# Loading the query and key stacks three groups ahead instead of two in a transformer kernel

## What is computed

```
x = x + cross_attention0(norm(x), ctx, mask)          # 16 heads of 16 features
x = x + block0(norm(x))     # self-attention (16 heads), then 8 experts of 1024 hidden units
x = x + cross_attention1(norm(x), ctx)                # no mask
x = x + experts1(norm(x))   # gate over 256 columns, 8 experts of 256 x 256
```

## Time and profile before

| | us |
|---|---|
| median of 3 runs (lowest, highest) | 1280.65 (1279.75, 1281.99) |
| the profiled execution's own time | 1274.43 |
| its span, first to last instruction | 1272.7 |
| TensorE busy | 1131.4 (89%) |
| VectorE busy | 838.6 (66%) |
| ScalarE busy | 660.4 (52%) |
| GpSimd busy | 210.9 (17%) |
| mean granted TensorE clock | 0.949 of full |

### The profile page before, as it was taken

One profiled execution on the slowest core, in us unless ns is written; L12 is line 12 of the kernel. 1 busy time (PEld: TensorE's weight loads), 2 busy tenths in 40 slices (PEclk: granted clock), 3 DMA queues, 4 the chain that ended last, 5 costly groups with the idle time before them and its releaser, 6 DMA issues. The chain is left out here.

```text
span 1272.7 us, 17810 instructions
## 1 busy us (share of the span) xinstructions
PE 1131.4 (89%) x5693; PEld 544.0 (43%) x5722; DVE 838.6 (66%) x2112; ACT 660.4 (52%) x1341; POOL 210.9 (17%) x272
## 2 busy tenths in 40 slices
PE   7889999999997999999967999996989999998390
PEld 4423343434453223343364666664523333335370
DVE  5878777777478888888762222223888888876722
ACT  3346666666533677677722333332537767674250
POOL 4310000000143000000202222211520010102154
PEclk9989999999999899999967999998989999999795
DMA  8953321221048433543291140103873323211064
GB/s 265 309 169 93 79 57 28 81 52 26 2 154 291 103 91 90 132 97 93 72 375 33 31 161 28 27 13 102 263 241 91 90 59 89 60 37 57 25 171 144
DMA packets 100706, 139.40 MB, mean 110 GB/s; under 512 B 8452, under 2 KB 82632, under 8 KB 99208
## 3 DMA queue, kind: packets, MB, share of 16 engines
q1 hardware_dynamic: 96536, 128.03, 33.6%
q0 software_dynamic: 4080, 10.23, 2.9%
HBM read 86.30 MB, written 52.17 MB: 109 GB/s over the span
## 5 line engine op out<-in xcount | busy, mean ns | idle before, releaser
L885 ACT ACTIVATE r<-ps 128x512 f32<-128x512 f32 x768 | 427.4, 600 | 211.9 <-PE ps L971 122.1
L377 DVE TENSOR_REDUCE m<-ps 128x1 f32<-128x512 f32 x512 | 320.9, 682 | 45.2 <-PE ps L958 44.9
L971 PE MATMUL ps<-r 99*128 99x512 bf16 x768 | 294.3, 388 | 5.6 <-ACT r L885 5.6
L958 PE MATMUL ps<-r 96*128 96x512 bf16 x720 | 280.9, 393 | 20.5 <-DVE m L377 7.0
L373 DVE CUSTOM_DVE_ANT_0 r<-ps,r 128x512 bf16<-128x512 f32 x256 | 170.2, 690 | 60.2 <-PE ps L958 59.6
L985 PE MATMUL ps<-r 128*32 128x512 f32 x1536 | 204.9, 605 | 4.9 <-ACT r L885 3.3
L971 PEld LDWEIGHTS ps<-r 99*128 99x128 bf16 x768 | 74.4, 98 | 211.7 <-ACT r L885 157.3
L958 PEld LDWEIGHTS ps<-r 96*128 96x128 bf16 x720 | 71.3, 99 | 105.9 <-DVE m L377 24.3
L861 POOL COPY r<-r 128x256 f32<-128x256 f32 x48 | 19.0, 399 | 542.1 <-PE ps L985 542.1
L1660 DVE COPY r<-ps 128x512 f32<-128x512 f32 x46 | 31.8, 691 | 91.9 <-PE ps L1707 91.9
L1707 PE MATMUL ps<-r 128*128 x184 | 87.8, 621 | 2.7 <-issue 0.4
(11 more groups left out here) (151 smaller groups left out, 1220.5 us busy)
## 6 DMA issues: line engine op xcount, KB each, us to landing
r<-q_parts SPq DMA_DIRECT2D x48, 384.0 KB, 5.2
r<-k_parts SPq DMA_DIRECT2D x48, 384.0 KB, 6.0
k_parts<-r SPq DMA_DIRECT2D x24, 384.0 KB, 3.3
q_parts<-r SPq DMA_DIRECT2D x24, 384.0 KB, 3.1
r<-in_w SPq DMA_DIRECT2D x16, 512.0 KB, 4.9
r<-in_w SPq DMA_DIRECT2D x8, 1024.0 KB, 14.4
k_parts<-r SPq DMA_DIRECT2D x24, 256.0 KB, 3.3
q_parts<-r SPq DMA_DIRECT2D x24, 256.0 KB, 3.1
```

Source lines behind the costliest of these rows:

```text
L377: ins = dve.tensor_reduce(out, mem.ps[:, bank, :], AX.X, ALU.max)
L885: act.activation(mem.probs[:, u // HG, u % HG, :], ps[:, ST + (UNITS * g + u) % DEEP, :], ACT.Exp, scale=SCALE).then_inc(a.p_exp.sem, 1)
L958: pe.matmul(ps[:, led_bank(n), :], mem.qst[g][0:ROWS, h, t * P:(t + 1) * P], mem.kst[g][0:ROWS, h, :], start=True, stop=True).then_inc(a.s ...
L971: ins = pe.matmul(out, mem.kst[g][0:KROWS, h, kt * P:(kt + 1) * P], mem.qst[g][0:KROWS, h, :], start=True, stop=not a.masked)
```

## The change

The stacks are loaded three groups ahead. In the projection phase a third group's stacks are loaded beside the first two. In the attention phase step 1 of group G loads the stacks of group G + 3; its wait is for the transposed scores of group G - 1, whose buffers these are, and for G = 0 there is no wait. So that step now comes when group G - 1 has ended, and the shift of group G + 1 is issued behind it. The wait for the last stores of the projection moves with it to g = 1 of the first batch. No load is added or left out over a stage.

```diff
         for n in range(QK):
             sp.wait_ge(a.stored[n].sem, a.stored[n].at(1))
-        load_stacks(sp, a, 0, 0)
-        load_stacks(sp, a, 0, 1)
+        for g in range(AHEAD):
+            load_stacks(sp, a, 0, g)
         body(B - 2, None)
         body(B - 1, None)
...
+AHEAD = 3
...
         for g in range(NG):
             G = NG * b + g
-            ahead = (b, g + 2) if g < 2 else (b + 1, g - 2)
-            if not (last and g >= 2):
-                if first and g == 2:
+            ahead = (b, g + AHEAD) if g + AHEAD < NG else (b + 1, g + AHEAD - NG)
+            if not (last and g + AHEAD >= NG):
+                if first and g + AHEAD == NG:
                     for n in range(QK):
                         sp.wait_ge(a.stored[n].sem, a.stored[n].at(B))
-                if not (first and g < 2):
-                    sp.wait_ge(a.st_ps.sem, a.st_ps.at(G - 1))
+                if G + AHEAD >= NG:
+                    sp.wait_ge(a.st_ps.sem, a.st_ps.at(G + AHEAD - NG + 1))
                 load_stacks(sp, a, *ahead)
```

## The result

| | before | changed |
|---|---|---|
| median, us (lowest to highest) | 1279.75 (1276.92 to 1281.99), 7 runs | 1284.56 (1283.51 to 1286.37), 7 runs |
| ratio, 95% interval | | 1.0040 (1.0026 to 1.0054) |
| span of the profiled execution, us | 1272.7 | 1282.2 |
| mean granted TensorE clock there | 0.949 | 0.945 |

The change costs 4.8 us in the medians. The two profiled executions lie 9.5 us apart, since that of before is one of its quicker ones; so the places are read from the profiles and the size from the medians. The page's engine row, which answers to the earlier trace rows: the same work. The 7 us more of busy TensorE are in part a gap in the record: the profile of before lacks 29 matmuls of its line 975 (x5693 against x5722), and two profiles of experiments 1 and 7, which have all 5722, show 1134.7 and 1135.3.

What follows compares the result with a forecast made beforehand. PE was taken to bound the attention phases and DVE the end of each projection phase. A gain of 5.2 us and a cost of 6.5 made +1.3, 1281.9 us from a median of 1280.65; whole range 1276.0 to 1286.5.

Steps and rivals of the forecast that it cites:

- all twelve waits go: Attention phases: loads issued 8 units sooner end all twelve waits of plain scores for the stack loads of line 334.
- the wait put into SP's queue: Attention phase, SP's queue: the new wait for the end of group G - 1 was put at nothing.
- the gain of 5.2 us: Attention phases: worth of the twelve removed waits, measured between matmul starts less cadence; bounds 3.4 and 7.6 us.
- Rival C: Attention phases: removed waits come back as waits for ACT or DVE; gain 2 us or less, time 1285, chance 0.15.
- the third pair's bytes hold up batch 2's stores: Projection phases: 768 KB ahead of the stores delay them 3.1 us a stage; 6.5 us together on the path.
- Rival A: Projection phases: the last batch's first-piece stores are not late, gain without cost; time 1275.4, chance 0.20.
- 11 us to land: Projection phases, a sign: stores behind the loads take about 11 us to land, 8.5 in the second stage.
- SP's longer issuing: Projection phases: two more DMAs, about 1.0 us to issue, costed at nothing; at most 1.0 a stage if engines run dry.
- rival B: Last projection batch: PE's clock falls in the pause, 5 to 7.5 us a stage; 1287 if in one stage; chance 0.13.
- the likeliest case: Whole kernel: the forecast itself, -5.2 + 6.5 = +1.3 us, 1281.9, own range 1277.5 to 1284.5, chance 0.52.
- "The same": Whole kernel: measured time within 0.2%, 2.6 us, of the kernel before; chance 0.42.
- "slower": Whole kernel: slower than the kernel before by over 0.2%, 2.6 us; chance 0.32.

Runs made afterwards that it cites:

- experiment 1: Changed kernel with the third pair of stacks loaded at the start of the attention phase, behind the first shift; 1275.29 us, ratio 0.9978 to the kernel before.
- experiment 7: Changed kernel with only the first pair of stacks ahead of batch 2's stores, second and third behind them; 1274.40 us, ratio 0.9973 to the kernel before.
- experiment 5: Against experiment 1's kernel: two loads of 24 KB each in the projection phase, in the early third pair's place; 1275.09 us, ratio 0.9977 to the kernel before.
- experiment 6: Changed kernel with the fourth group's stacks also loaded in the projection phase, no load at group 0; 1294.56 us, ratio 1.0132 to the kernel before.
- experiment 3: Changed kernel with TensorE doing the last batch's second key projection twice, to fill the pause; 1279.41 us, ratio 1.0009 to the kernel before.
- experiment 8: Experiment 7's kernel with the third plain score ahead of each attention phase issued 13 times; 1275.22 us, ratio 0.9977 to the kernel before.

## Why the prediction was right in part and wrong in part

- **Right: all twelve waits go.** Line 334 has no plain score waiting, and the wait put into SP's queue costs nothing (experiment 1).
- **Mis-sized: the gain of 5.2 us.** It measured 3.84 from group 1 on in the profiles and 2.8 in the medians of experiment 1. I had written that the start of the matmuls "say when the work behind can go". They do not: each wait removed uncovers about 0.2 us of waiting for DVE's bank. Rival C, that the waits come back, is true for a quarter of the gain in the profiles and for nearly half of it by the medians.
- **Right: the third pair's bytes hold up batch 2's stores, and ACT, then DVE, wait for them in all three stages.** The awaited store landed 2.9 and 3.1 us later in stages 1 and 3, against the 3.1 of a pair. Rival A, that the stores are not late, falls. Experiments 5 and 6 bear out size and dose. For the wait alone 2.45, 1.4 and 2.7 were expected, 6.5 together; the changed kernel shows 2.01, 1.66 and 2.98, 6.65. One sign did not come: the stores did not take 11 us to land, since most of the delay was in their issue. SP's longer issuing was costed at nothing beside the loads, and as the landings moved by no more than 3.1, nothing of it shows on top.
- **Wrong: the clock.** I gave rival B 0.13, holding against it that the clock stayed up over 920 to 922, with PE short of work there too. It fell in two of three stages and cost 3.2 us in the profiles, 1.33 and 1.89; the filler of experiment 3 took 2.9 of it away, and gave 4 in the medians, whose interval holds both. This term, put at nothing in the sum, and the gain that was 1.4 to 2.4 us too large turned a forecast of +1.3 into +4.8. B's price of 5 to 7.5 us a stage was too high: two or three steps were to run at the low clock, and one did, DVE's wait of 1.79 us being its price in stage 3. The Trainium skill (TensorE: Matmul & The Clock Gate, What's actually happening) says that half rate is the default and that activity releases the clock. The changed kernel's windows agree: 0.50 after the pause, and 1.00 in experiment 3 with the pause filled.
- With the measured sizes the sum closes roughly: -3.8 + 6.65 + 3.2 is +6.0 against the 4.8 to 5.1 of the medians.

The forecast of 1281.9 was 2.7 us low; the time lies within the whole range and just outside the likeliest case's own, 1277.5 to 1284.5. There is some luck in that. The change itself was forecast at +1.3 and measured at +4.8; the forecast stood on a median of three runs, 1280.65, which over seven runs is 1279.75, and those 0.9 us bring it nearer. "The same" had the highest chance, 0.42, and "slower", which came, 0.32. The time is also nearly that of rival C, 1285, by other terms: C had the gain 3.2 us short and no clock, and the profiles have it 1.4 short and the clock at 3.2.

## What to carry to other kernels

A prefetch moved earlier is moved in front of something, so look first at what stands behind it in the same queue and whether the DMA engines have room there: here the later loads could move ahead for nothing, and the third early pair belonged behind the stores that someone waits for (for the second pair no difference is shown). And where a wait on the path makes TensorE pause, read the granted clock behind the pause: its fall added 3.2 us here to a wait of 6.65. Cut a difference between two profiles at the point where each cause can first act; only so did it show that part of what the filler seemed to gain lay ahead of it.

## What the runs showed of the hardware that I had not expected

- A pause of 2.80 us of TensorE in the last batch, after a stretch at full clock, was followed by a granted clock of 0.50; in stage 1 the changed kernel's shorter ones (54 to 60 us, busy 1.17 to 1.77 of each 2) were not.
- The clock fell without a long pause too, in experiment 8 at 938 to 940 us, where PE was busy 1.42 of the 2 us before.
- More matmuls made a kernel faster: 4 in each stage, 1.88 us of added work a stage, for some 4 us of the whole; without the pause the same 4 cost 2.7 us.
- Each pair of 384 KB loads that was put ahead of stores in a full queue (DMA share 1.10 to 1.12, 246 to 254 GB/s over 920 to 926 us in the changed kernel) made the start of ACT's first piece 1.7 to 4.3 us later, 2.4 on the mean of three stages for the third pair and 3.1 for the fourth; for the third, most of it was in when SP issued the store and not in its time to land.
